# Edge stage of a graph layer: VectorE's comparisons gathered into one operation, its additions into four

## What is computed

```python
xn  = layernorm(x)                                  # 6250 x 256
msg = relu(xn[src] + edge_attr)                     # 106250 x 256
agg = zeros_like(xn).at[dst].add(msg)               # dst is sorted
h   = xn + agg                                      # goes on into the MLP of the layer
```

## Time and profile before

| | |
|---|---|
| median of three runs | 2364.78 us (2362.48 to 2366.32) |
| the profiled execution | 2375.34 us, its span 2373.7 us |
| edge stage, first gather to the end of the last additions | 71.3 to about 1315 us |
| POOL busy in the whole program | 1185.4 us (50%), 851.7 us of it in 832 gathers |
| DVE busy | 1259.5 us (53%): 258.9 us in 832 comparisons, 344.5 us in 832 additions |
| PE busy | 1814.1 us (76%), ACT 821.0 us (35%) |
| granted clock of TensorE, mean | 0.853 |

### The profile page before, as it was taken

The page is one execution under the profiler, slowest core; times in us unless marked ns, Lnnn a source line. Parts: engine busy times, 40 slices in busy tenths (PEclk is TensorE's granted clock), DMA queues, the critical chain, the costliest instruction groups (busy, mean ns, idle before and its releaser), DMA issues. The chain is left out here.

```text
span 2373.7 us, 35031 instructions
## 1 busy us (share of the span) xinstructions
PE 1814.1 (76%) x10022; PEld 1438.5 (61%) x10023; DVE 1259.5 (53%) x3894; ACT 821.0 (35%) x1704; POOL 1185.4 (50%) x1121
## 2 busy tenths in 40 slices
PE   4266666666657767787787698876499999999996
PEld 3254444455545444554554587765488888888885
DVE  7355454555545555555555376656844444444442
ACT  4122222222222222322222256573044444444442
POOL 1576676676776766676766000022034444444443
PEclk8578777877777897888888799955899999999998
DMA  7555555655555566656655265466512222222322
GB/s 242 177 188 191 188 190 163 205 181 194 186 189 187 183 199 204 203 195 201 203 195 184 87 210 179 166 200 238 195 38 46 47 48 45 45 45 45 47 46 33
DMA packets 142031, 356.40 MB, mean 150 GB/s; under 512 B 33130, under 2 KB 79625, under 8 KB 127611
## 3 DMA queue, kind: packets, MB, share of 16 engines
q0 software_dynamic: 66624, 157.12, 25.6%
q1 hardware_dynamic: 69068, 198.31, 23.6%
q10 hardware_dynamic: 6255, 0.10, 0.3%
HBM read 297.49 MB, written 57.94 MB: 150 GB/s over the span
## 5 line engine op out<-in xcount | busy, mean ns | idle before, releaser
L189 POOL DMA_INDIRECT gathered<-xn_rows,src_table x832 | 851.7, 1024 | 389.9 <-issue 261.4
L817 PE MATMUL bank<-edge_attr,dst_select 128*128 128x256 f32 x1664 | 543.5, 496 | 336.5 <-ACT edge_attr L731 169.9
L817 PEld LDWEIGHTS bank<-edge_attr,dst_select 128*128 128x128 f32 x1664 | 416.4, 257 | 459.5 <-issue 217.1
L621 DVE TENSOR_SCALAR dst_select<-iota_window,dst_partition 128x128 f32<-128x128 f32 x832 | 258.9, 312 | 466.5 <-DMA gathered<-xn_rows,src_table 384.6
L731 ACT ACTIVATE edge_attr<-edge_attr 128x2048 f32<-128x2048 f32 x104 | 198.6, 1910 | 758.4 <-DVE edge_attr L632 474.6
L1821 PE MATMUL bank<-rowsT_parts,expert_weights 128*128 128x256 f16 x3564 | 409.2, 274 | 10.1 <-issue 6.3
L1821 PEld LDWEIGHTS bank<-rowsT_parts,expert_weights 128*128 x3564 | 346.8, 98 | 59.0 <-issue 18.1
L632 DVE TENSOR_TENSOR edge_attr<-gathered,edge_attr 128x256 f32<-128x256 f32 x832 | 344.5, 415 | 0.0
L1782 POOL DMA_INDIRECT out<-expert_out,output_row_of_slot x108 | 183.3, 1697 | 301.6 <-ACTq L1880 279.1
L1927 DVE SCALAR_TENSOR_TENSOR gated<-bank,silu 128x512 f32<-128x512 f32 x216 | 120.7, 559 | 184.8 <-ACT silu L1866 173.6
L1834 PE MATMUL bank<-expert_weights,gated_parts 128*128 x1836 | 209.3, 273 | 0.4 <-DVE gated_parts L1935 0.4
(11 more groups left out here) (274 smaller groups left out, 1939.3 us busy)
## 6 DMA issues: line engine op xcount, KB each, us to landing
edge_attr<-in_edge_attr SPq DMA_DIRECT2D x104, 1024.0 KB
raw_weights<-in_L_ffn_w SPq DMA_DIRECT2D x32, 544.0 KB, 4.6
expert_weight_parts<-weight_parts SPq DMA_DIRECT2D x32, 544.0 KB, 3.1
expert_weights<-expert_weight_parts SPq DMA_DIRECT2D x8, 2176.0 KB, 25.2
gathered<-xn_rows,src_table POOLq DMA_INDIRECT x832
rows_in<-xn_rows SPq DMA_DIRECT2D x48, 128.0 KB
rows_in<-in_x SPq DMA_DIRECT2D x48, 128.0 KB
residual_rows<-residual_tile SPq DMA_DIRECT2D x48, 128.0 KB
```

What stands on the lines that cost most here:

```text
L189: pool.indirect_dma_start(out=k.GA[h][:, e, :], out_offset=None, in_=k.xn_d[:, :], in_offset=bass.IndirectOffsetOnAxis(ap=k.src[:, b, e:e ...
L621: dve.tensor_scalar(SEL[b % 3][:, e, :], k.iota[:, :], k.dstp[:, b, e:e + 1], None, ALU.is_equal)
L817: last = pe.matmul(WINP[j % 2][:, 0:C], SEL[j % 3][:, e, :], EA[j % 3][:, e, :], start=e == 0, stop=e == EK - 1)
```

## The change

The eight comparisons of a batch become one `tensor_tensor` of 1024 columns, whose two inputs are the window positions, repeated over the eight edge columns, and the eight numbers per partition, each repeated 128 times. It stands behind the additions instead of between them, and has its own wait on `win_full` (for the same value as before). The eight additions of 256 columns become four of 512. What VectorE computes is the same.

```diff
@@ edge_mix_stage @@
+    ADDED = 2
...
         @block.vector
         def _(dve):
-            def select(b, e):
-                dve.tensor_scalar(SEL[b % 3][:, e, :], k.iota[:, :], k.dstp[:, b, e:e + 1], None, ALU.is_equal)
+            def select(b):
+                if b > 1:
+                    dve.wait_ge(win_full, b - 2)
+                dve.tensor_tensor(SEL[b % 3][:, :, :], k.iota[:, :].unsqueeze(1).to_broadcast([128, EK, WIN]),
+                                  k.dstp[:, b, :].unsqueeze(2).to_broadcast([128, EK, WIN]), ALU.is_equal)
 
             def add(b):
                 ea, ga = EA[b % 3], GA[b % 2]
                 dve.wait_ge(ea_in[b % 3], 16 * (b // 3 + 1))
                 dve.wait_ge(g_in[b % 2], 16 * EK * (b // 2 + 1))
-                if b > 1:
-                    dve.wait_ge(win_full, b - 1)
-                for e in range(EK):
-                    if b + 1 < NB:
-                        select(b + 1, e)
-                    last = dve.tensor_tensor(ea[:, e, :], ga[:, e, :], ea[:, e, :], ALU.add)
+                for e in range(0, EK, ADDED):
+                    last = dve.tensor_tensor(ea[:, e:e + ADDED, :], ga[:, e:e + ADDED, :], ea[:, e:e + ADDED, :], ALU.add)
                 last.then_inc(added, 1)
+                if b + 1 < NB:
+                    select(b + 1)
...
-            for e in range(EK):
-                select(0, e)
+            select(0)
             for b in range(NB):
                 add(b)
```

## The result

The changed kernel takes 2395.4 us (median of 4 runs, 2390.56 to 2399.0), the kernel before 2364.45 beside it: a ratio of 1.013 [1.011, 1.015], slower by 31 us. I had forecast 2611 us; the sign was right, the size was not.

What follows compares the result with a forecast made beforehand. POOL's gathers and idle time bound the edge stage (1241.6 us). Longer holds +250 and earlier `added` -4 gave +246 on the profiled 2375.3, or 2611 us against the median; range 2380 to 2660, its own 2560 to 2660.

Steps and rivals of the forecast that it cites:

- POOL is the chain of the stage: Edge stage: POOL's 832 gathers and the idle time before them make up the whole stage, 1241.6 us.
- Four additions in 2.40 us, the comparison in 1.22, `added` 1.85 us earlier behind the batch's start: VectorE's piece of a batch: falls from 4.26 to 3.53 us, with `added` at 2.5 us instead of 4.34.
- DVE's saved work: VectorE in the edge stage: 76 us less work, all in front of waits for gathers, worth 0 us.
- The hold of one operation is 0.54 for 512 columns and 1.06 for 1024: POOL's gathers beside VectorE: an addition or the comparison holds a gather this many us behind its start.
- So I take the hold as one piece.: Additions and comparison of a batch: hold gathers without a gap until 3.46 us behind the batch's start; +250 us.
- rival 1: Edge-stage gathers: POOL gets in at every end of a VectorE operation; 41 us, 2402 us; chance 0.17.
- ReLU and scatter start 1.85 us earlier, with nobody short of them: Behind the additions: earlier `added` saves only POOL's 4 waits for it, at most 7 us, taken as 4.
- The wait for `win_full` costs nothing: Before the comparison: the wait moved there is for a scatter two batches old; 0 us.
- Rivals 2 and 3: POOL gets in only between additions and comparison, 2495 us, chance 0.15; plain additions leave POOL alone, 2295 us, chance 0.13.
- rival 3: Edge-stage gathers: comparisons between the additions kept POOL out, so a row of additions frees it; 2295 us; chance 0.13.

Runs made afterwards that it cites:

- h runs: Four kernels on one chip: changed kernel 2387.57 us, with four 256-column comparisons 2346.51, that plus late edge load 2327.31, eight small additions then eight small comparisons, late load 2330.36.
- e4: Kernel before with four additions of 512, each behind two small tensor_scalar comparisons; 2400.60 us, ratio 1.0178.
- e1: Changed kernel with its comparison taken back to eight tensor_scalar, behind the four additions; 2401.49 us, ratio 1.0171.
- h1: Changed kernel, unchanged, measured a second time on another chip; 2387.57 us, ratio 1.010.
- h3: Changed kernel with the comparison as four tensor_tensor of 256 columns, measured again on another chip; 2346.51 us, ratio 0.9922.
- f1: Changed kernel with a later edge load: batch b's load also waits until batch b-2's gathers have landed; 2348.84 us, ratio 0.9953.
- g1: Kernel before with the late edge load of f1 added; 2354.29 us, ratio 0.9963.
- e3: Changed kernel with eight additions of 256 in a row, then eight small tensor_scalar comparisons; 2419.25 us, ratio 1.0232.
- i1: The kernel of e3, unchanged, measured again on another chip; 2335.21 us, ratio 0.9886.
- g3: e3 with the comparisons moved behind the key and scaling pieces, plus the late edge load of f1; 2404.82 us, ratio 1.0189.
- g4: e1 with the late edge load of f1 added; 2404.23 us, ratio 1.016.
- e2: Changed kernel with eight additions of 256 and the wide comparison kept; 2408.04 us, ratio 1.0206.

## Why the prediction was right or wrong

- *POOL is the chain of the stage.* Right. Its sum grew by 20.2 us and the stage with it, and among the h runs the median follows the sum.
- *Four additions in 2.40 us, the comparison in 1.22, `added` 1.85 us earlier behind the batch's start.* Right: the comparison took 1219 ns and started 2.47 us behind the first addition, and the last addition ended at 2.54 in place of 4.34. DVE's saved work was worth nothing, as said.
- *The hold of one operation is 0.54 for 512 columns and 1.06 for 1024.* Right: 0.57 and 1.09 in the batch shown.
- *"So I take the hold as one piece."* This step failed. It carried +250 us; the measured term is +8.7. What the runs show is the mechanism of rival 1: in the changed kernel each of 184 held gathers got in at the end of the operation that it began beside. The evidence for my step was two gathers that lost to an addition with a `tensor_scalar` ahead of it, and e4 shows that this is a case of its own. Where operations of one form follow each other POOL gets in between them, but for the 30 gathers named above. The additions' share of the holding fell from 65 us to about 30 (e1), and the comparison brought some 40 (h1 against h3, 35, with four narrow ones still in it).
- *Rival 1's size.* It had 41 us for the holding, not 8.7. The batches in which POOL wakes with VectorE have 0.90 us in the mean, its 0.91; the others have 0.53, where it had 1.1. That its 2402 us lie close to 2395 is luck: what it had too much in the holding, the loads took. The range down to 2380 held the result only through rivals 1 and 2.
- *"ReLU and scatter start 1.85 us earlier, with nobody short of them"*, put at -4 us. This step failed in sign. What waited for the scatter was SyncE's edge load, which I had left out: of a step that is moved the DMAs behind it count too. The loads came earlier, into the gathers' transfers; the stops of POOL grew by 10.5 us and its waits for landings by 25.5, and f1 takes both back (16 us and 105.1). POOL's waits for the additions, of which I took 4 us, fell by 19.9, but with TensorE's slow batches and not by the change. With the late load the changed kernel (f1, 0.9953) and the kernel before (g1, 0.9963) are level, within their intervals, and so nearly are their POOL sums (1213.0 and 1218.8 us). So the loss of the change is the loads' timing; its own operations about break even.
- *The wait for `win_full` costs nothing.* Right: the comparison's group shows 16.7 us of idle time, all of it before the stage's first batch.
- *Rivals 2 and 3.* No gather was held until the comparison, and the additions do hold gathers with no comparison between. But a part of rival 3 is true: the comparisons between the additions made the holding worse. In e3 and i1, without them, 25 to 27 us were left of 65.

## What to carry to other kernels

Where GpSimd's indirect DMAs are the chain, count for each VectorE operation with two inputs in SBUF how long it holds a gather (here 0.29, 0.57 and 1.09 us for 256, 512 and 1024 columns), since that is what one gather can lose to it; keep such operations short and in a row, and put the `tensor_scalar` work elsewhere. Then look at the longest gathers, for a row that held as one piece (g3). When an edit makes a semaphore come earlier, follow it to the DMAs that it releases: a big load that starts earlier can land in the way of the transfers that are waited for. And measure a surprising loss again on another chip before explaining it.

## What the runs showed of the hardware

- An indirect DMA's issue is held by a `tensor_tensor` with both inputs in SBUF until 0.29 us behind its start at 256 columns, 0.57 at 512 and 1.09 at 1024, and let in then even if the next one follows at once (3219 gathers against 30). Of 829 that began within 0.04 us behind the operation's start, 687 went free. One that begins beside a `tensor_scalar` directly in front of a `tensor_tensor` is mostly held through both (1.68 us in place of 0.94 in e4).
- POOL stopped before the second gather of batches 15, 29, 43 and so on in every kernel, 112 gathers of 128 rows apart, for 1.7 us at best and up to 6.1 where large loads were under way. What is full there was not tried.
- On two of five chips TensorE had stretches in which it issued its products with gaps of up to 2.4 us (g4), in five of eight kernels, worth 70 to 95 us in the three that were measured again. What sets them off stays open; e2, e4 and g1 ran on the same chips without. The profile of the kernel before has one such batch, of 11.4 us, and single gaps in two others.
